# Deformable sampling in strips of two pixel rows: one tap per step, all four groups on the partitions, three blocks of products per image

## The reference, cut to what matters

```
x = x + _L0_conv_ref(_gn(x), ...)            # local attention
om = conv3x3(_gn(x), w_om) + b_om            # 4*9*(dy, dx, mask) per pixel
py = h - 1 + ki + dy ; px = w - 1 + kj + dx
v = bilinear sample of group d of _gn(x) at (py, px), zero outside, times sigmoid(mask)
x = x + relu(einsum('ogck,bgckhw->bohw', w_dcn, v))
```

## Time and profile before

| | us |
|---|---|
| median of 3 runs | 250.47 (248.32 to 252.61) |
| profiled execution, whole | 250.16 |
| its span, first to last instruction | 248.1 |
| PE busy | 207.7 (84%) |
| DVE busy | 178.8 (72%) |
| POOL busy | 134.3 (54%) |
| ACT busy | 129.0 (52%) |
| sampling, from the first multiply to the last copy out | about 110 to 237 |

### The profile page before, as it was taken

How to read it: one execution, slowest core, us unless ns; L and a number is a source line. 1 busy time by engine, 2 the same in 40 slices (tenths; PEclk the granted TensorE clock), 3 DMA queues, 4 the chain that set the end, 5 groups by cost and what they waited for, 6 DMA issues and landing times.

```text
span 248.1 us, 4924 instructions
## 1 busy us (share of the span) xinstructions
PE 207.7 (84%) x1906; PEld 117.5 (47%) x1906; DVE 178.8 (72%) x233; ACT 129.0 (52%) x240; POOL 134.3 (54%) x167
## 2 busy tenths in 40 slices
PE   0687789989899996929897998979979899899844
PEld 0324443953335662316454655546646456555520
DVE  1499978897674575078886896887868868789724
ACT  1142038300015629746888686896778867865000
POOL 9409942999000004816769477585776766964000
PEclk9999999999999998995999999999999999999987
DMA  6920000000300111101000000000000000000003
GB/s 227 211 17 0 3 0 0 4 0 3 77 7 0 45 34 37 49 9 45 4 0 3 0 4 0 4 0 3 3 0 3 0 3 3 3 0 5 7 8 85
DMA packets 9976, 5.59 MB, mean 23 GB/s; under 512 B 6887, under 2 KB 8805, under 8 KB 9945
## 3 DMA queue, kind: packets, MB, share of 16 engines
q1 hardware_dynamic: 9657, 4.30, 7.3%
q10 hardware_dynamic: 288, 0.89, 1.1%
HBM read 2.82 MB, written 0.52 MB: 13 GB/s over the span
## 4 chain that ended last, share of the span: by engine, by line
PE 56%; ACT 13%; DVE 12%; issue 9%; POOL 6%; DMA 2%; SPq 0%; ACTq 0%; DVEq 0%; POOLq 0%
PE ps L1066 10%; PE ps L1040 9%; PE ps L970 9%; DVE smp_prod L654 6%; PE ps L1024 5%; ACT hx_selx L543 4%; ACT disty L532 4%; PE ps L863 3%; PE ps L1082 3%; PE ps L1097 3%; PE ps L987 3%; DMA x_parts<-in_x 2%; PE ps L1103 2%; PE ps L928 2%; POOL smp_prod L362 2%
## 5 line engine op out<-in xcount | busy, mean ns | idle before, releaser
L763 DVE TENSOR_TENSOR smp_prod<-ps,hx_selx 128x1024 f32<-128x1024 f32 x72 | 87.1, 1222 | 13.4 <-PE ps L1040 11.7
L543 ACT ACTIVATE hx_selx<-ps 128x512 f32<-128x512 f32 x72 | 42.5, 591 | 24.0 <-PE ps L1024 23.2
L390 POOL TENSOR_SCALAR disty<-disty 64x512 f32<-64x512 f32 (+1 forms) x24 | 13.2, 548 | 43.6 <-ACT haty L535 42.8
L1024 PE MATMUL ps<-stack_x,selx 110*128 110x256 bf16 x144 | 28.9, 283 | 5.1 <-ACT hx_selx L543 4.8
L403 POOL TENSOR_SCALAR hx_selx<-hx_selx 128x512 f32<-128x512 f32 x32 | 19.6, 613 | 19.5 <-ACT hx_selx L543 17.9
L1040 PE MATMUL ps<-haty,bcast 128*128 128x256 f16 x160 | 25.2, 281 | 5.0 <-DVE smp_prod L763 4.1
L1066 PE MATMUL ps<-smp_prod,windows_attention 128*32 128x192 f32 x512 | 27.0, 332 | 0.0
L546 ACT ACTIVATE hx_selx<-hx_selx 128x512 f32<-128x512 f32 x40 | 25.2, 631 | 1.3
L395 POOL TENSOR_TENSOR haty<-disty,haty 64x512 f16<-64x512 f32 (+1 forms) x24 | 23.9, 994 | 2.0
L970 PE MATMUL ps<-conv_staged 128*108 128x512 f32 x48 | 24.5, 619 | 0.0
L406 POOL TENSOR_SCALAR hx_selx<-hx_selx 128x512 f32<-128x512 f32 x32 | 19.8, 618 | 2.6
(11 more groups left out here) (121 smaller groups left out, 346.6 us busy)
## 6 DMA issues: line engine op xcount, KB each, us to landing
x_parts<-in_x SPq DMA_DIRECT2D x2, 256.0 KB, 5.3
x2seq<-x_parts SPq DMA_DIRECT2D x2, 256.0 KB, 3.7
out<-x2seq SPq DMA_DIRECT2D x4, 128.0 KB, 2.3
vals_attw<-in_cf ACTq DMA_DIRECT2D x1, 480.0 KB, 6.0
stack_x<-x_parts SPq DMA_DIRECT2D x12, 36.0 KB
stack_y<-x_parts SPq DMA_DIRECT2D x12, 36.0 KB
stack_m<-x_parts SPq DMA_DIRECT2D x12, 36.0 KB
kept<-in_cf ACTq DMA_DIRECT2D x1, 390.5 KB, 4.3
```

Of the source, the lines that this page charges most:

```text
L543: nc.scalar.activation(h, bank(5), ACT.Abs).then_inc(s_absx, 1)
L763: nc.vector.tensor_tensor(four, rows, cols.unsqueeze(2).to_broadcast([P, 2, 2, HW]), ALU.mult).then_inc(s_mult, 1)
L1024: ins = nc.tensor.matmul(bank(5)[:, k * HW:(k + 1) * HW], selx2[:, at:at + P], stack["x"][:, i * HW:(i + 1) * HW], start=True, stop=True)
```

## The change

- A strip is 2 pixel rows and needs 6 image rows, which are three pairs of rows. A pair of rows times 16 columns times 4 groups is 128 partitions, so all groups fit at once, and a step is one tap: three `spread_y` matmuls instead of four, 768 columns on DVE instead of 1024.
- `select_x` works on units of two taps, every second step (36 units instead of 72), with `selx` itself as weights; ACT makes both parts of the hats (`hat_x`), and POOL's `minus_hat_x` is gone. The multiply by -1 (`minus_by`) is gone as well.
- An image has 3 blocks of products: in step 6 (taps 0 to 5, strips 0 to 3), step 8 (taps 0 to 5, strips 4 to 7) and step 1 of the next image (taps 6 to 8). A block has 10 or 11 products of 128 x 64 on one half of PE's columns, the two halves alternating, of 96, 192 or 288 columns. DVE's `values` stand after steps 7, 0 and 2.
- The pixels are staged with the groups apart: `staged[partition, row, group, x]` is `tall` times a 0/1 mask of the channel's own group, 1408 columns per image; DVE does image 0, POOL images 1 to 3, each one instruction. The transposes read `staged` (128 x 128 instead of 128 x 64), there are 17 groups instead of 15, and each is copied out with one 128 x 512 copy. The memset of the window area is gone.
- On POOL, two copies of 384 columns (`by_rows`) replace `minus_by` (1024 columns), and the four `selx2` copies are gone. On DVE a reduction for the group mask and six one-column memsets stand before `b2half`. Eight small DMAs become one.

```
-STRIP = 4
+STRIP = 2
+ROWS = STRIP + 2 * REACH
+QUARTERS = ROWS // 2
...
+            def stage(j, shift):
+
+                at = shift * (ROWS * W)
+                rows = images(tall)[:, j, bass.ds(at, SROWS * W)].rearrange("p (r x) -> p r x", r=SROWS)
+                nc.gpsimd.tensor_tensor(staged_image(j), rows.unsqueeze(2).to_broadcast([P, SROWS, DG, W]), group_mask(SROWS),
+                                        ALU.mult).then_inc(s_staged, 1)
+
+            pool.wait_ge(s_own, 1)
+            pool.wait_ge(s_tall, J)
+            for j in range(1, J):
+                stage(j, CENTER)
...
+            rows = images(tall)[:, 0, ROWS * CENTER * W:(ROWS * CENTER + SROWS) * W].rearrange("p (r x) -> p r x", r=SROWS)
+            nc.vector.tensor_tensor(staged_image(0), rows.unsqueeze(2).to_broadcast([P, SROWS, DG, W]), group_mask(SROWS),
+                                    ALU.mult).then_inc(s_staged0, 1)
...
                         if k == 2:
-                            pe.wait_ge(s_tall, J)
+                            pe.wait_ge(s_staged0, 1)
+                            pe.wait_ge(s_staged, 1)
...
-                four = smp[:, r:r + 2 * BANK].rearrange("p (k q n) -> p k q n", k=2, q=2)
+                pairs = smp[:, r:r + WIDE].rearrange("p (q n) -> p q n", n=HW)
...
+            def products(i, tiles, dst, it):
+
+                lists = [needed(i, ki, side, it) for ki, side in tiles]
+                for m in range(SIDE + 2):
+                    for n, (ki, side) in enumerate(tiles):
+                        at = side * SIDE + m
+                        if at in lists[n]:
+                            ins = product(i, ki, at, side, dst[n * C:(n + 1) * C], at == lists[n][0], at == lists[n][-1])
+                ins.then_inc(s_chunk, 1)
...
-                    if t + LEAD < T:
-                        select_x(t + LEAD, it)
+                    if t % 2 == 0 and t // 2 + LEAD < UNITS:
+                        select_x(t // 2 + LEAD, it)
...
-                    if m >= 6:
+                    if m in UPPER:
...
-                    if i and m == 0:
-                        upper_taps(i - 1, 3, it)
-                    if i and m in (1, 2):
-                        lower_taps(i - 1, m - 1, it)
+                    if i and m == LOWER:
+                        lower_taps(i - 1, it)
```

More of the change, by code:

```diff
@@ L55, with groups @@
 MASKS = {0: {4: 0, 8: 1}, 1: {0: 2, 2: 3, 4: 4, 8: 5}}
[L56 removed]
+CHUNK, VALS, SLICES = 3, 3, 6
 SEL_Y = {1: 0, 3: 1, 7: 2}
+UPPER = {6: 0, 8: 1}
+LOWER = 1
 FINAL = 5
[L61 to L70 removed]
+def groups(it):
+    return GROUPS[isinstance(it, int)]
 def seventh(i, m):
@@ new lines, in strips_with, with product @@
+            def strips_with(m, side):
+                first = max(side * SIDE, m - 2)
+                return first, min(side * SIDE + SIDE - 1, m) - first + 1
+            def product(i, ki, m, side, dst, start, stop):
+                first, strips = strips_with(m, side)
+                rows, inner = pair_of_rows(i, ki, m)
+                at = (first - side * SIDE) * 3 * SP
+                return nc.tensor.matmul(dst[:, at:at + strips * 3 * SP].rearrange("p (s k n) -> p s k n", k=3, n=SP), rows,
+                                        sampled(i, ki, m, first, strips), start=start, stop=stop, skip_group_check=True)
@@ new lines, in needed @@
+            def needed(i, ki, side, it):
+                return [m for m in range(side * SIDE, side * SIDE + SIDE + 2)
+                        if not isinstance(it, int) or pair_of_rows(i, ki, m)[1]]
+            def products(i, tiles, dst, it):
[6 more added lines that the diff above has]
+                ins.then_inc(s_chunk, 1)
```

397 lines of the change are left out of this document (168 added, 229 removed).

## The result

| | before | after |
|---|---|---|
| median of 20 runs each, us | 250.69 (248.32 to 253.28) | 254.0 (250.72 to 259.06) |
| ratio | | 1.010 (95% interval 1.007 to 1.013) |
| profiled execution: time, span, us | 250.16, 248.1 | 256.2, 253.6 |

The changed kernel is slower, by 1.0% or 2.5 us: clear of noise, and inside the two per cent to which I had given a chance of 0.32. I had forecast 257.5, 7 us more than before: the direction was right, the size nearly three times too large. The times of the changed kernel spread over 8 us, and on the whole the longer an execution is, the lower is its mean granted clock; the ratio is made only from executions at most 1.5% above the fastest of the same kernel, so it leaves out those that lost most to the clock, and the plain medians give 1.013. The profiled execution lost clock at three of the eight finals of sampling.

The account below looks back on a forecast made before the run. PE was taken to bound the steps with blocks, ACT's short instructions the stretch before `final`. On 250.16: -3.0 + 0.4 + 0.3 + 6.3 + 2.5 + 1.7 - 0.4, less 0.8, gave 257.2, as median 257.5; range 247 to 263.

Parts of the forecast that it names:

- The stall at group 5: Ahead of sampling, PE's fifth transpose group waits for a DVE copy held up by POOL's stagings: +6.3, half clock +2.5; chance 0.52.
- Ahead of attention: Seven small DVE instructions before `b2half` cost +0.7, of which shorter `by_rows` copies on POOL return some: +0.4 us.
- The memset: Without it POOL's L362 starts earlier, but DVE's first L683 falls inside it: between -0.4 and +1.2, taken as +0.3 us.
- my own walk: POOL and DVE in turn from 73.6 us, stagings 3.3 us each, ending with the copy of group 1 at 88.6 or 88.7.
- The low end that I had kept: At group 5, if only DVE's two subtractions were held up, the copy would end at 84.4: +2.1 us.
- Eight more transposes with wide weights: Ahead of sampling, 68 transposes instead of 60, taken at 0.12 us each with 128-column weights: +1.7 us.
- Filling: One select and one distance fewer while the pipelines fill: -0.4 us.
- Sampling: Cheaper spreads and selects against dearer blocks and longer waits: period 16.3 against 16.1 us, -3.0 us in all, bounds -7.8 and +3.4.
- The rival with cheap overhead: Sampling's blocks: at the skill's 60 cycles per matmul, 32 products instead of 48 win 0.8 us per image, 6.4 in all.
- Rival 2: No stall at group 5: POOL lets DVE in between or takes under 2 us per instruction; 249.5 us, chance 0.20.

Follow-up runs that it names:

- the kernel where POOL yields: On the changed kernel, POOL waits with its second and third staging until DVE has split the first offsets; ratio 0.9945, median 250.62 us.
- the fastest one: Changed kernel with POOL's staging wait, third block in step 4, and second half of the x hats on POOL; ratio 0.962, median 240.56 us.

## Why the prediction was right or wrong

Two steps failed. The stall at group 5, 8.8 us in my sum with its half clock, was 4.95, above all because I took a staging on POOL to be 3.3 us where it is 2.4. And the half clock in sampling, which I put at nothing, cost 5.6 us in the profiled execution. That this execution, 256.2, came within 1 us of my 257.2 is luck: the terms of my sum were 6.5 us too slow in all, and the loss that I left out is 5.6.

**Ahead of attention**, forecast +0.4: measured -1.05 (first bias at 33.91 instead of 34.96). The small instructions of DVE are pipelined to next to nothing, one of the DMAs landed 0.35 earlier (in the execution with the memset back, with the same code up to there, it didn't), and I had seen the shorter copies of POOL only as something that returns a part. They seem to have given more: DVE's twelve products took 13.3 instead of 14.2, which fits with POOL holding them up less, but no run varied that alone.

**The memset**, forecast +0.3, up to +1.2: the mechanism was right and the size +0.8. The rows that answer to the earlier trace rows, after:

```profile
45.47 5.38 POOL L363 TENSOR_TENSOR smp_prod<-smp_prod,windows_attention 128x1024 f32<-128x1024 f32 x2 [12.96 <-ACT smp_prod L478]
...
46.46 2.31 DVE L666 TENSOR_TENSOR smp_prod<-smp_prod 128x1024 f32<-128x1024 f32 x1
...
51.07 3.29 DVE L666 TENSOR_TENSOR smp_prod<-smp_prod 128x1024 f32<-128x1024 f32 x1
```

POOL starts 2.6 us earlier, and both sums of DVE are inside its instructions; the lead of 1.05 us at the start is 0.2 at the second normalisation. The kernel with the memset back confirms the 0.8.

**The stall at group 5**, forecast +6.3 and +2.5 at half clock: the place, the order of the engines and the row that PE waits for came out as written, but 3.2 and about 1.75 us. The step that failed is the rate of POOL. I took 2.35 us per 1024 columns from an in-place sum, so 3.3 for a staging. Measured: the three take 8.95 us, of which POOL itself waited 1.39 for DVE's own staging and 0.43 for the cast, which leaves 2.4 each, 1.7 ns a column where the sum takes 2.3 (in the kernel where POOL yields, the last two take 2.5 each). With 2.4 in my own walk POOL ends 2.7 us earlier, at 83.5, and the copy of group 1 starts at 85.2 instead of 87.9: that is +3.6 instead of +6.3, so the rate explains nearly the whole error. The copy started at 84.7 in fact, and two of DVE's instructions were held, the cast by the second staging and the subtraction by the third, where my walk had a short wait for the cast and whole ones for two others. The half clock I had put at 5 us long and 2.5 dear; it cost 1.75 of the 4.8 us from 85.46 to 90.23. The low end that I had kept (+2.1, only the subtractions) was below the truth, the value taken above it.

The Trainium skill ("SBUF — State Buffer", section "SBUF: two separate sides") says that a DVE instruction with two SBUF inputs or in a mode with two ports, and a GpSimd instruction, exclude each other for the whole instruction. This case agrees: 0.43 becomes 2.79 and 0.69 becomes 2.90, and with halved stagings 0.69 becomes 1.73.

**Eight more transposes with wide weights**, forecast +1.7 less 0.8: they take 0.108 each as before (four from 90.23 to 90.67), so +0.9. The wider weights are hidden; 0.12 was too much and the sum was right.

**Filling**, forecast -0.4: measured -1.1 (15.35 us from the third offsets to the first multiply, against 16.44). A part of this is no gain of the change: the kernel before ran at a granted clock of 0.60 between 96 and 100, where two products of a convolution step took 1.92 us, and the changed kernel at 1.00 between 96 and 110, where they took 1.02. How the 1.1 divides wasn't separated.

The five terms make -1.05 + 0.8 + 3.2 + 1.75 + 0.9 - 1.1 = +4.5, and the first multiply is 4.4 us later. I had forecast +10.0.

**Sampling.** The step costs were right nearly everywhere: multiplies 0.95 forecast, 0.953 measured; blocks 2.06, 2.22 and 2.22 forecast, 2.04, 2.2 and 2.2 measured with their start; a period of 16.3 forecast, 16.0 at full clock. From the lower block to the final I had 5.9 in every image; it is 5.7 in every second one (145.97 to 151.63) and 4.8 in the others (130.94 to 135.72), so the rest of the period, 10.4 forecast, is 10.8 on average, and two errors cancel in part. One reading of the rows was wrong: ACT is relieved of 3.0 us per image and not of 1.6 (42.5 + 25.2 before, 21.2 + 22.7 after, for eight images); the sum didn't use it. Up to the first final -3.4, and -4.0 to the last, where I had -3.0. The finding that work taken off DVE brings nothing held.

What I missed is the clock. I had found that PE would wait longer before each final, and I had a row that showed what a wait does, and used it at group 5 alone. There are 2.3 us of waits in two pieces in the image that ends at 151.63, and 1.5 in the next. At 1.2 GHz a `final` takes 2.8 us instead of 1.5 (151.63 to 154.44), and behind the third one the next block takes 2.75 instead of 1.94 until the clock is back. In the profiled execution this cost 5.6 us: 2.0, 1.0 and 2.7 at the three finals. Without it that execution would have taken 250.6, next to the fastest one measured, 250.72, and 0.4 above the 250.16 of the kernel before: so between these two executions nearly the whole slowdown is the clock's, since the +4.4 ahead of sampling and the -4.0 - 0.4 in and behind it cancel. The kernel before has its own losses to the clock, though: its fastest execution, 248.32 at a mean granted clock of 0.983, lies 1.8 us below the profiled one (0.970), and fastest against fastest the changed kernel is 2.4 us slower. My forecast came out on the right side with a stall that was too large by 3.8 us, and a loss in sampling that it left out.

The Trainium skill ("TensorE: Matmul & The Clock Gate", section "A second HAM failure mode: psum-queue depth-cycling") describes a kernel in which short idle times between groups of matmuls, from banks that go to and fro, make the clock swing between its levels. This case agrees in kind: waits of 0.76 and 1.56 us, both for bank 7, which goes to and fro between PE and ACT, are followed by a final of 1.54 us instead of 0.86. It is the rule I should have weighed beside the longer stretch before `final`.

**The rival with cheap overhead** fell: the 11 products of a later block (22 instructions in the trace), 1152 columns of time, stand in 2.10 us, of which the columns are 1.92; the 10 of the first stand in 1.94, of which 1.76. What is left, 0.18 for both, leaves room for no price per product that 32 instead of 48 could save much of. Rival 2 (249.5) needed stagings under 2 us or an engine that lets the other in between, and neither came; its time is near what the kernel where POOL yields came to, 250.6 in the median, with 246.6 in its profiled execution.

## What to carry to other kernels

Where PE waits for another engine in every turn of a loop, the price isn't the wait alone: the clock may fall behind it, in some turns and some executions. Look at what each engine passes between two dependent steps, and move real work of PE into that stretch (here one block, from step 1 to step 4); matmuls without use keep the clock too and cost more than they give when they are not wholly inside the wait. And before POOL is given an instruction, find every two-input or fast DVE instruction that will fall beside it and who waits for that: an order of DVE's own instructions, or a wait on POOL, was worth 4 to 5 us at the first final here.

## What the runs showed of the hardware

- One instruction type has two rates on POOL: products with broadcast inputs into another tile took 1.7 to 1.8 ns a column (2.4 to 2.5 us per 1408), the in-place sum 2.3 (2.35 per 1024). I don't know which property decides it; no kernel here varied it alone.
- The same wait of 3.2 us ahead of group 5 was followed by a convolution step of 1.42 us in the changed kernel and of 1.02 with the memset back, and equal waits in sampling (1.14 for ACT, then three spreads) by 0.82 in one image and 0.50 in another of the same execution. What decides between them wasn't settled. It makes the spread of a kernel's times a sign to read: 8 us for the changed kernel, with granted clocks from 0.971 (250.72 us) to 0.933 (259.06), 5 us for the kernel before, and 0.9 us for the fastest one, all at 0.968 to 0.978.
- Float32 transposes of 128 columns run at 0.108 us each with weights of 128 columns, as those with 64 did before.
